# GNN and product-key layers on one core: a landing semaphore for each gather slot, and a request that waits for the one three places ahead

## The reference, cut to what matters

```
q = (x @ Wq + bq).reshape(-1, 8, 128)            # 8 heads, two halves of 64
s1, s2 = q1 . keys[:, 0], q2 . keys[:, 1]        # 256 scores each
s1t, i1 = top_k(s1, 8);  s2t, i2 = top_k(s2, 8)
scores, best = top_k(all 64 sums s1t + s2t, 8)
indices = i1 * 256 + i2  at best                 # 64 rows for each node
w_d, w_u = w_down[indices], w_up[indices]        # from tables of 65536 x 512
inner = einsum('bd,bhkd->bhk', x, w_d)
out = einsum('bhk,bhkd->bd', relu(inner) * softmax(scores), w_u)
```

## Time and profile before

| | us |
|---|---|
| median of 3 timed runs | 1168.22 (1167.57 to 1169.13) |
| span of the profiled execution | 1265.9 |
| first request issued | 216.3 |
| last request issued | 1139.9 |
| GpSimd, 628 requests, busy | 593.8 |
| TensorE, line 2098, busy | 603.1 |
| VectorE, line 1531, busy | 491.2 |

### The profile page before, as it was taken

The page is one execution under the profiler, slowest core; times in us unless marked ns, Lnnn a source line. Parts: engine busy times, 40 slices in busy tenths (PEclk is TensorE's granted clock), DMA queues, the critical chain, the costliest instruction groups (busy, mean ns, idle before and its releaser), DMA issues.

```text
span 1265.9 us, 15265 instructions
## 1 busy us (share of the span) xinstructions
PE 1116.7 (88%) x3706; PEld 585.9 (46%) x3707; DVE 865.3 (68%) x2769; ACT 441.3 (35%) x1091; POOL 680.0 (54%) x758
## 2 busy tenths in 40 slices
PE   7999996498988798999988999989899987999898
PEld 3578894344443343444443444434444433444443
DVE  7657766477886766867867878768769674755621
ACT  4711134232533423433424424324334232432031
POOL 2200015655566665666666666667666666668312
PEclk9989998699999899999998999999999999999899
DMA  8940022989799999999999999999999999995632
GB/s 326 407 171 2 2 100 62 351 290 350 272 361 371 354 370 374 350 371 358 356 369 354 361 362 352 373 376 346 374 356 358 387 349 377 351 350 213 231 112 76
DMA packets 108664, 380.49 MB, mean 301 GB/s; under 512 B 11946, under 2 KB 12624, under 8 KB 108452
## 3 DMA queue, kind: packets, MB, share of 16 engines
q0 software_dynamic: 92352, 334.49, 70.9%
q1 hardware_dynamic: 16228, 45.04, 9.7%
HBM read 352.14 MB, written 28.46 MB: 301 GB/s over the span
## 4 chain that ended last, share of the span: by engine, by line
PE 53%; DVE 19%; issue 13%; another core or an unknown queue 4%; POOL 3%; ACT 2%; DVEq 2%; DMA 2%; SPq 1%; POOLq 0%; ACTq 0%
PE tr L2098 25%; DVE big L1531 8%; PE acc L1878 6%; PE acc L1990 4%; PE tr L2190 4%; PE acc L1949 4%; POOL big L701 3%; DVE AT L1531 2%; PE acc L1809 2%; PE acc L1960 2%; DVE topi L1397 2%; PE acc L1832 1%; PE tr L1982 1%; SPq L594 1%
## 5 line engine op out<-in xcount | busy, mean ns | idle before, releaser
L701 POOL DMA_INDIRECT big<-in_wdu,idx x504 | 476.8, 946 | 280.5 <-issue 133.0
L2098 PE MATMUL tr<-big,back 128*128 128x512 f32 x1008 | 486.3, 619 | 70.4 <-issue 41.6
L1531 DVE CUSTOM_DVE_ANT_0 big<-big,acc,prob 128x512 f32<-128x512 f32 x504 | 350.6, 743 | 11.9 <-DMA big<-in_wdu,idx 6.0
L2098 PEld LDWEIGHTS tr<-big,back 128*128 128x128 f32 x1008 | 190.3, 196 | 319.8 <-issue 272.6
L1039 ACT ACTIVATE back<-ident,inner 128x128 f32<-128x128 f32 x576 | 197.0, 396 | 381.7 <-DVE inner L1531 117.1
L701 POOL DMA_INDIRECT AT<-in_wdu,idx x124 | 117.0, 943 | 62.0 <-issue 33.2
L2098 PE MATMUL tr<-AT,back 128*128 128x512 f32 x248 | 116.8, 598 | 12.1 <-issue 11.2
L1878 PE MATMUL acc<-AT,big 128*128 128x256 f32 (+1 forms) x400 | 90.9, 379 | 0.0
L1531 DVE CUSTOM_DVE_ANT_0 AT<-AT,acc,prob 128x512 f32<-128x512 f32 x124 | 86.6, 742 | 5.2 <-issue 4.2
L1990 PE MATMUL acc<-front 128*128 128x512 f32 x188 | 90.1, 604 | 0.0
L1949 PEld LDWEIGHTS acc<-front 128*128 128x128 f32 x640 | 79.2, 197 | 19.1 <-issue 18.2
(11 more groups left out here) (334 smaller groups left out, 1082.9 us busy)
## 6 DMA issues: line engine op xcount, KB each, us to landing
sorted_rows<-big SPq DMA_DIRECT2D x33, 640.0 KB, 18.7
big<-in_we SPq DMA_DIRECT2D x8, 1024.0 KB, 14.1
big<-in_wdu,idx POOLq DMA_INDIRECT x504
x<-sorted_rows SPq DMA_DIRECT2D x14, 257.5 KB, 2.6
x<-in_x SPq DMA_DIRECT2D x1, 2304.0 KB
big<-in_xt SPq DMA_DIRECT2D x2, 1024.0 KB, 8.9
front<-in_wq SPq DMA_DIRECT2D x1, 2048.0 KB, 7.8
AT<-in_wdu,idx POOLq DMA_INDIRECT x124
```

What stands on the lines that cost most here:

```text
L701: pool.indirect_dma_start(out=k.slot[r * GS + s], out_offset=None, in_=k.wdu_d, in_offset=bass.IndirectOffsetOnAxis(ap=k.idx[i % 2][:, j:j ...
L1531: ins = dve.tensor_tensor_reduce(out=row, in0=row, in1=k.Y[i % 2] if i < NT - 1 else k.Yh[j // WIDTH], scale=k.prob[:, (i % 2) * HK + j:(i ...
L2098: ins = pe.matmul(k.O[i % 2], k.diag[:, c:c + P], row, start=(g == 0 and s == 0), stop=(g == groups_of(i) - 1 and s == GS - 1))
```

## The change

Each of the 20 slots gets its own landing semaphore. GpSimd, before it issues request m (counted over all tiles), waits until request m - 3 has landed; it still waits for the group that used the slots before. VectorE waits for one slot before each of its two instructions of line 1531, and no longer for both before the first. What is fetched, into which slots and in which order stays as it is.

```diff
--- before.py
+++ after.py
@@ -70,6 +70,8 @@
 SHARES = 2
 NG = HK // GS
 RING = 10
+SLOTS_HELD = RING * GS
+AHEAD = 3
 SPARE = P - LAST
 HELD = -(-LAST // SPARE)
 WIDTH = -(-HK // (HELD + 1))
@@ -520,7 +522,7 @@
         k.x4_seen = sem("x4_seen")
         k.loaded = [sem(f"loaded{r}") for r in range(XR)]
         k.stored = [sem(f"stored{r}") for r in range(XR)]
-        k.landed = [ctx.enter_context(nc.semaphore(f"landed{r}")) for r in range(RING)]
+        k.landed = [sem(f"landed{m}") for m in range(RING * GS)]
         k.x_d, k.xt_d, k.src_d, k.dst_d, k.w0t_d, k.par_d, k.wq_d = x_d, xt_d, src_d, dst_d, w0t_d, par_d, wq_d
         k.zs_d = nc.dram_tensor("sorted_rows", (PLACES * P, ROW), F32).ap()
         k.keys_d, k.wdu_d, k.w1_d, k.b1_d, k.we_d, k.out_d = keys_d, wdu_d, w1_d, b1_d, we_d, out_d
@@ -698,10 +700,13 @@
             pool.wait_ge(k.grp_done, n + 1)
             for s in range(GS):
                 j = g * GS + s
+                m = n * GS + s
+                if m >= AHEAD:
+                    pool.wait_ge(k.landed[(m - AHEAD) % SLOTS_HELD], ((m - AHEAD) // SLOTS_HELD + 1) * 16)
                 pool.indirect_dma_start(
                     out=k.slot[r * GS + s], out_offset=None, in_=k.wdu_d,
                     in_offset=bass.IndirectOffsetOnAxis(ap=k.idx[i % 2][:, j:j + 1], axis=0),
-                ).then_inc(k.landed[r], 16)
+                ).then_inc(k.landed[r * GS + s], 16)
 
     def add_b1(t):
         pool.wait_ge(k.x2_flipped, t + 1)
@@ -1524,9 +1529,9 @@
                     dve.wait_ge(k.y_kept, i + 1)
                 else:
                     dve.wait_ge(k.y_hosted, 2)
-            dve.wait_ge(k.landed[r], (n // RING + 1) * (16 * GS))
             for s in range(GS):
                 j = g * GS + s
+                dve.wait_ge(k.landed[r * GS + s], (n // RING + 1) * 16)
                 row = k.slot[r * GS + s][:, 0:D]
                 ins = dve.tensor_tensor_reduce(
                     out=row, in0=row, in1=k.Y[i % 2] if i < NT - 1 else k.Yh[j // WIDTH],
```

## The result

The changed kernel takes 1548.67 us (median of 4 runs, 1547.90 to 1550.98), the kernel before on the same chip 1168.68 us (4 runs, 1167.57 to 1169.27). The ratio is 1.3252, 95% interval 1.3236 to 1.3267. The forecast was 1300 us with a range up to 1420: the direction was right, but the change that was forecast, 131 us, is a third of the measured 380.

What follows compares the result with a forecast made beforehand. Transfers, with TensorE close behind, were taken to bound the gathers. At 1.60 us, 563 steps take 901 us, not 814 (+87), last trip -2: 1351 us profiled; timed 1247 or 1351, middle 1300 us, own range 1225 to 1380, outer 1195 to 1420.

Steps and rivals of the forecast that it cites:

- the stops: GpSimd's 3.46 us pauses between gather requests, once in 16 to 20, could add up to 0.2 us per request.
- That is five in flight: Queue depth before the change, from the last request's 6.72 us to VectorE's start at 1.25 us per request.
- The bound on requests in flight: Gather stage: waiting for request m-3 makes the pace (trip + reaction) / 3, taken as 1.60 us, +87 us over 563 steps.
- tight bound, 1.77 us: Rival, gathers: trip stays 5.0 us or stops add in full; 1447 us profiled, 1335 to 1447 timed; chance 0.17.
- loses nothing: First gather tile, 216 to 326 us: already at 1.69 us per request, slower than 1.60, so no added time.
- all parts shrink alike: Profiled to timed: every part scales by 0.923, so 1351 us becomes 1247 us.
- the difference lies in the stage: Profiled to timed: the 97.7 us gap lies in the stage from 326 us on; bound's 901 us stay, giving 1351 us.
- The waits themselves: GpSimd's 625 added waits: taken as 0 us, at most 0.30 us each.
- VectorE's wait for each slot: VectorE's 314 added waits and its 0.67 us earlier start on a pair's first slot: both taken as 0.
- will idle more: TensorE in the gather stage: 665 us of work, 758 at clock 0.86, fits within 819 us, so no cost.
- Loose bound: Rival, gathers: issue to reaction under 4.34 us, so pace unchanged and time 1168 us; chance 0.08.
- A shallower queue frees the others: Rival, gathers: three in flight remove VectorE's idle time and GpSimd's stops; pace 1.33 us, 1201 us profiled; chance 0.09.

Runs made afterwards that it cites:

- the undisturbed recording: The kernel before the change, unedited, recorded a second time: 1170.82 us (one run).
- the distances 1 to 4: Changed kernel with AHEAD, how many places back the awaited request lies, at 1, 2, 3 (the change itself), 4: 3347.08, 1980.12, 1548.67, 1353.62 us.
- distance 1: Changed kernel with AHEAD set from 3 to 1, so one request at a time: 3347.08 us (one run).
- the disturbed recording: First recording of the unedited kernel before the change, the one the prediction read: span 1265.9 us, against 1168.22 us timed.
- distance 20: Changed kernel with AHEAD set from 3 to 20, all waits kept but none holding anything up: 1168.51 us, ratio 0.9998 to the kernel before.
- distance 3: The changed kernel itself, AHEAD = 3, against the kernel before: 1548.67 us, ratio 1.3252.

## Why the prediction was right in kind and wrong in size

**What binds now.** Wrong in part. From the earlier trace rows the prediction saw a queue that carries the transfers at 408 GB/s, and that held; but it took the pace of 1.443 us, with its stops, for the kernel's. Undisturbed it is 1.28, and the 0.2 us that the stops were to add at the upper end are not there either. "That is five in flight", read from one late place, was too low: the line of the requests shows a median trip of 10.2 us in the undisturbed recording, eight in flight at 1.28. This changed nothing in "it binds".

**The bound on requests in flight, the step that failed.** Its form, (trip + reaction) / 3, is what the chain shows, and the distances 1 to 4 fit it. Both numbers in it were too small.
- The trip was taken as 4.5 us; it is 5.2. Both ends, 3.7 and 5.0 us, were read from the time at which the bytes stop. The landing counts 0.5 us later, as the trip of distance 1 shows (4.2 alone, 3.7 to the last byte). With the same 0.5 added, an estimate, the place taken between the two ends becomes 5.0 and the upper end 5.5: most of the miss is the landing, and the rest is that three in flight lie nearer to the upper end than was taken. 0.7 / 3 x 563 = 131 us.
- The reaction was taken as 0.30 us, GpSimd's gap between two requests that wait for nothing. That row holds no landing. It is 0.26 where the wait sits in the request and 0.78 where it is an instruction of its own, 0.52 on average. 0.22 / 3 x 563 = 41 us.

That is why "tight bound, 1.77 us", the upper end, was passed too: it had 5.0 + 0.3 where 5.2 + 0.52 belonged. The 5.31 us that seemed to support it hold VectorE's reaction, which is 0.02 to 0.03 us in the chain of the changed kernel, and not GpSimd's. Their trip, 5.28 us, was the right one: with 0.52 it makes a pace of 1.93.

**The first tile "loses nothing".** Wrong: 1.69 us came from the disturbed recording. Undisturbed, the 110 us hold 74 requests, 1.486 each, and 58 after, 1.897. Over 64 requests that is 0.411 x 64 = 26 us.

**How that stands to the median.** Of the two readings, "all parts shrink alike" (1247) and "the difference lies in the stage" (1351), the second was right in the main: the gathers were the disturbed part (12 us of it lay ahead of the second tile), and the bound's time did not shrink. The middle that was taken, 1300, gave away 51 us.

Together: 1300 + 51 + 131 + 41 + 26 = 1549, and 1548.67 was measured. That close a match is luck. From the first request of the second tile to the last request the undisturbed kernel took 726 us (314.25 to 1040.21), not the 716 of the prediction, which takes 10 us off the loss; and the changed kernel took 1081 us (339.21 to 1420.52), 1.921 a step and not 1.907, which adds 8.

**The waits themselves and VectorE's wait for each slot, both at 0.** Right: ratio 0.9998 at distance 20.

**TensorE "will idle more", the clock costs nothing.** Right: busy 540.90 of 739 us, granted clock 0.95 (time at 2.4 mixed with time at 1.2 GHz), and the landings still set the pace.

**The rivals.** "Loose bound" fell: distance 3 costs 33%. The Trainium skill's formula, on which it drew, gives 3.2 us, an estimate, and misses the trip by 1 us alone and 2 us with three in flight. "A shallower queue frees the others" fell: the stops whose end was to pay for it do not belong to the kernel, and no distance is faster than the kernel before.

**The signs.** Idle time before requests released by DMA, DMA under 0.92 and 340 GB/s (0.83, 274), VectorE's landing waits over 50 us (284), TensorE under 84% (77): all came, though VectorE's landing waits are 111 us in the undisturbed kernel already. Requests 1.5 to 1.8 us apart did not; they are 1.91 apart.

## What to carry to other kernels

A limit of n requests in flight makes the pace (issue to landing + landing to next issue) / n, with the trip taken under that very load and up to the landing, not to the last byte; n must reach the time of that round, read at that n, divided by the time that one transfer takes when the queue is full (here (6.9 + 0.52) / 1.28 = 5.8, six). Where an instruction has several waits, see in the chain which of them becomes an instruction of its own, and let it not be the late one. Before pricing a stage from a recording that is 8% longer than the timed runs, look which stretches hold idle time without a cause: their paces are not the kernel's.

## What was not expected of the hardware

- The trip grows with the number in flight long before DMA is full: 4.2, 4.7, 5.2 and 5.8 us for one to four, at 110, 200, 274 and 327 GB/s. Why is left open.
- DMA's busy share is not its use: 0.37 at 110 GB/s and 0.83 at 274, but 1.03 at 408, there for 674 us on end and not in short stretches only. By the share alone distance 3 would have 24% to gain; by the bytes it had 49%.
- A landing wait that is an instruction of its own costs 0.52 us more than one in the request (0.78 against 0.26). What fills the 0.72 us behind it no view shows.
- With one request in flight TensorE, busy for 306.53 of 674 us, was granted 0.66 on average, and the short stretches above stand at 0.50, the 1.2 GHz level; with DMA full it was granted 1.00.
